# Four of sixteen scan inputs built by ScalarE and TensorE, more read-outs on GpSimd, and the z projection moved ahead of the gate

## The chip, the core and the metric

The kernel runs on one core of a Trainium2 chip. Five engines execute their own instruction streams and meet at semaphores: TensorE (PE in the profile, its weight loads PEld), VectorE (DVE), ScalarE (ACT), GpSimd (POOL) and SyncE (SP, which issues most DMAs). The metric is the device time of one execution in microseconds (us), lower is better. Before the change, three runs gave 1917.44, 1918.84 and 1922.55 us (median 1918.84).

## The reference, cut to what matters

Two layers, each a mixing block and a feed-forward block, work on x of shape (4, 256, 32, 32): 4 batches of 1024 tokens with 256 channels. The part that the change touches is the first mixing block. It cuts the 256 channels into 4 chunks of 64 and runs a state-space scan with 128 inner channels and 16 states over the 1024 tokens of each chunk of each batch:

```
xi, z = split(x @ in_proj.T);  xc = silu(causal_conv4(xi))
dbc = xc @ x_proj.T;  B, C = dbc[4:20], dbc[20:36]          # 16 numbers each per token
dt  = softplus(dbc[0:4] @ dt_proj.T + bias);  A = -exp(A_log)
h_t[d,s] = exp(dt_t[d] * A[d,s]) * h_(t-1)[d,s] + (dt_t[d] * xc_t[d]) * B_t[s]
y_t[d]   = sum_s h_t[d,s] * C_t[s];   out = ((y + xc * D) * silu(z)) @ out_proj.T
```

Behind it stand a projection, a quantized feed-forward layer, a group norm with channel attention, and at the end, over all 4096 tokens, a mixture of 8 experts with 2 chosen per token.

## The kernel before, in words

The program has three parts: four batches one after the other, then the routing, then the experts. A batch b has a stage of scans; the stage between two batches finishes batch b-1 (projection to gate) and begins batch b (convolution, dt, B and C, z). The first batch has a stage `start` in place of this.

**A scan.** Channels lie on the 128 partitions, the 1024 tokens along the free axis. One chunk has 16 states, a batch 64, numbered i = 0 to 63 (chunk i // 16, state s = i % 16). For each state four things are made, each of 128x1024 fp32: ScalarE writes the decay exp(dt * A) into PSUM (`decay`, L1002; two slots); GpSimd multiplies dt * xc with the row B[s], which SyncE has broadcast to all partitions by a DMA from the DRAM scratch `bc_rows` (`drive`, L1090; the product is called a drive here, three slots, the row buffers have four); VectorE runs the recurrence over both (`tensor_tensor_scan`, L1401; three state slots); then the state is multiplied with the row C[s] (the read-out, two slots `HC`) and TensorE adds the product into a PSUM bank by a matmul with the identity (`sum_states`).

**Read-outs** of states 2, 6, 10 and 14 are done by GpSimd with a C row broadcast by a DMA (L1098). The other twelve are done by VectorE (L1411) with a C row that TensorE spreads over the partitions into the one PSUM buffer `crep`: two bf16 matmuls (`c_row`) with a selector against `BCS`, which holds C as three bf16 parts that add up to the fp32 value. GpSimd makes these parts (`split_bc`), and SyncE copies them into place with 12 DMAs (`spread_bc`).

**Order.** Each engine runs its own list, written by loops over i. VectorE: scan i, at s = 1 and 2 of a later chunk the gating and the skip sum of the chunk before, read-out i-1. GpSimd: drive i, read-out i-2 where it is its own; beside that a few steps for dt of chunks 2 and 3 (`steps_of_dt`, after drives 2 and 8), a small norm step that waits for VectorE (`first_shift`, i = 35), and four bias sums (`residual`). TensorE: `c_row(i)`, `sum_states(i-1)`. ScalarE: decay i, then pieces of the norms of the last and the next batch. SyncE: row i of B, row i of C for GpSimd, and at i = 8 and 10 the store of the previous batch's tokens, a wait for it, and the load of the next batch.

**Between batches.** TensorE ends with `out_linear`, two transposes of the tokens (`tm_turn`), the gate's matmuls (`gate`) and only then the projection of z (`z_pair`, two halves). ScalarE runs the silu of z (`silu_z`, L829) inside the scans, after decay 1, which waits for the gate's logits (`gate_done`). VectorE computes `log1p` for chunks 0 to 3, the last one behind the logits (`route`). TensorE begins the scans when all of silu(z) is there.

Of the kernel before, what the change touches and what calls it, by code (L numbers as in the profile page):

```python
# [8 lines left out]
BF16 = mybir.dt.bfloat16  # L9
# [16 lines left out]
POOL_READS = (2, 6, 10, 14)  # L26
# [31 lines left out]
def on_pool(i):  # L58
    return i % NS in POOL_READS

# [27 lines left out]
def build_front(nc, t, out, xm_rows, bc_rows, logits, routing, experts):  # L88
    with ExitStack() as ctx:
# [76 lines left out]
        diag_d = shared(P)  # L166
        ffn_w = shared(CT, C)
# [16 lines left out]
        YF = shared(L)  # L184
        assert place[0] <= LAST_W2
# [36 lines left out]
        BC_REST = flat_rows(junk)  # L222
# [32 lines left out]
        dt_done = sem("dt_done"); dtx_done = sem("dtx_done"); bc_copy = sem("bc_copy"); bc_split = sem("bc_split"); bc_spread = sem("bc_spread")  # L255
        brow_ready = sem("brow_ready"); brow_stored = sem("brow_stored")
        b_loaded = [sem(f"b_loaded{k}") for k in range(B_SLOTS)]
        drive_ready = sem("drive_ready"); da_ready = sem("da_ready"); h_ready = sem("h_ready")
        crep_ready = sem("crep_ready"); c_loaded_rows = [sem(f"c_loaded_rows{k}") for k in range(2)]
# [5 lines left out]
        stats_there = sem("stats_there"); rest_there = sem("rest_there"); tokens_there = sem("tokens_there")  # L265
# [34 lines left out]
        def _(sp):  # L300
# [56 lines left out]
            for i in range(NI):  # L357
# [48 lines left out]
        def _(pe):  # L406
# [1617 lines left out]
```

## Time and profile before

| | |
|---|---|
| median of the runs shown | 1918.84 us |
| the profiled execution | 1918.7 us, its span 1916.9 us |
| scans of batches 0 to 3 | 83.9 to 296.1, 394.8 to 611.5, 712.9 to 929.0, 1030.3 to 1246.0 us |
| stages between | 98.7, 101.4, 101.3 us |
| after the last scan, to the first expert matmul | 1246.0 to 1396.8 us |
| experts | 1396.8 us to the end, PE busy 508.63 of 520.10 us |
| busy over the span | PE 79%, DVE 66%, POOL 60%, ACT 40% |

A scan stage is counted here from the start of the first scan to the end of the last read-out. In the second batch its chunks begin at about 394.8, 452.7, 504.9 and 558.7 us. In a row of windows the columns are start and end, length, then busy us of PE, PEld, DVE, ACT and POOL (in brackets the instructions), TensorE's granted clock as a share of its 2.4 GHz, the DMA engines' mean busy share and GB/s. In a timeline row the columns are start, duration, engine, line, operation, tiles, and in brackets the idle time ahead of it and what ended that. Many tiles share one SBUF buffer, which the trace calls `experts_sb`. A transpose on TensorE is a matmul of line 411; an fp32 matmul shows as two records.

### The profile page before, as it was taken

The page shows a single profiled execution, that of the slowest core. Times are in us where ns is not written, and L with a number is a line of the kernel's source. Part 1 is how long each engine was busy: PE and PEld are TensorE (multiplying, and loading weights), DVE is VectorE, ACT ScalarE, POOL GpSimd, SP SyncE. Part 2 cuts the span into 40 slices and gives each one's busy share as a digit, 9 for nine tenths or more (in the row PEclk, how much of TensorE's full clock was granted, in tenths as well). Part 3 has the DMA queues.
Part 4 walks back from the last instruction along what each step waited for, and adds up shares of the span by engine and source line. Part 5 has one row for each costly group of instructions (what it writes and reads, how often), then busy time and mean ns, then how long its engine had stood idle before and what let it go on. Part 6 is the DMA issues. An engine that isn't in the chain of part 4 may idle for free. (4 is left out here: it accounts for less than half of the span.)

```text
span 1916.9 us, 20726 instructions
## 1 busy us (share of the span) xinstructions
PE 1523.3 (79%) x5841; PEld 932.5 (49%) x5842; DVE 1258.3 (66%) x1415; ACT 772.8 (40%) x1218; POOL 1144.1 (60%) x602
## 2 busy tenths in 40 slices
PE   5567778957777877777896777767289999999997
PEld 2222225612223542222453222245178888888897
DVE  3589997589998678999848999963822222222222
ACT  7735435744443764543385344332022212222122
POOL 0799880479896068989217999800055455555543
PEclk9799999979999989999998999988589999999999
DMA  3365540146563036565004755481012222222222
GB/s 99 133 238 196 197 176 1 60 177 254 178 217 101 1 131 233 193 204 200 26 12 150 285 195 200 143 350 55 15 39 39 33 39 38 33 38 38 35 32 28
DMA packets 80689, 230.64 MB, mean 120 GB/s; under 512 B 12845, under 2 KB 31606, under 8 KB 77271
## 3 DMA queue, kind: packets, MB, share of 16 engines
q1 hardware_dynamic: 64694, 210.93, 31.1%
q0 software_dynamic: 15904, 18.66, 6.1%
q8 instruction: 38, 0.62, 0.1%
q14 instruction: 53, 0.43, 0.1%
HBM read 208.15 MB, written 19.82 MB: 119 GB/s over the span
## 5 line engine op out<-in xcount | busy, mean ns | idle before, releaser
L408 PE MATMUL psum<-HC_sb,ident_sb 128*128 128x512 f32 x1024 | 502.3, 616 | 98.7 <-DVE HC_sb L1411 50.2
L1002 ACT ACTIVATE psum<-experts_sb 128x1024 f32<-128x1024 f32 x256 | 285.2, 1117 | 492.4 <-DVE experts_sb L1401 363.5
L408 PE MATMUL psum<-experts_sb 64*128 64x512 f32 (+5 forms) x962 | 308.1, 551 | 180.1 <-DVE HC_sb L1411 100.2
L1401 DVE TENSOR_TENSOR_SCAN experts_sb<-psum,DBX_sb 128x1024 f32<-128x1024 f32 x172 | 389.8, 2278 | 36.9 <-POOL DBX_sb L1090 26.7
L408 PEld LDWEIGHTS psum<-HC_sb,ident_sb 128*128 128x128 f32 x1024 | 190.7, 194 | 323.6 <-issue 134.3
L408 PEld LDWEIGHTS psum<-experts_sb 64*128 64x128 f32 (+5 forms) x962 | 97.1, 153 | 418.6 <-DVE HC_sb L1411 191.3
L1817 ACT ACTIVATE hgt_sb<-psum_moe,b_sb 128x256 f32<-128x256 f32 (+1 forms) x312 | 116.2, 455 | 380.2 <-PE psum_moe L1724 380.2
L1969 DVE TENSOR_TENSOR YS_sb<-psum_moe,b_sb 128x256 f32<-128x256 f32 x71 | 30.2, 425 | 354.4 <-PE psum_moe L1724 354.4
L1724 PE MATMUL psum_moe<-XGT_sb,w1s_sb 128*128 128x256 f32 (+1 forms) x1248 | 254.7, 363 | 0.0
L1701 POOL DMA_INDIRECT out<-YS_sb,scat_sb x71 | 130.8, 1842 | 204.5 <-DVE YS_sb L1973 189.3
L1724 PE MATMUL psum_moe<-experts_sb,hgt_sb 128*128 x1136 | 251.7, 379 | 0.7 <-DVE YS_sb L1969 0.7
L1411 DVE TENSOR_TENSOR HC_sb<-psum,experts_sb 128x1024 f32<-128x1024 f32 x192 | 230.6, 1201 | 17.9 <-PE psum L408 17.7
L1724 PEld LDWEIGHTS psum_moe<-XGT_sb,w1s_sb 128*128 128x128 f32 x1248 | 219.4, 192 | 25.5
L1724 PEld LDWEIGHTS psum_moe<-experts_sb,hgt_sb 128*128 128x128 f32 x1136 | 215.2, 190 | 30.1 <-issue 1.1
L1090 POOL TENSOR_TENSOR DBX_sb<-DA_sb,experts_sb 128x1024 f32<-128x1024 f32 x88 | 209.7, 2385 | 7.0 <-DMA DA_sb<-bc_rows 7.0
L1401 DVE TENSOR_TENSOR_SCAN experts_sb<-psum,SQ_sb 128x1024 f32<-128x1024 f32 x84 | 191.1, 2275 | 2.9 <-POOL SQ_sb L1090 2.9
L1056 POOL TENSOR_TENSOR experts_sb<-experts_sb 128x1024 f32<-128x1024 f32 x16 | 38.6, 2412 | 243.3 <-DVE XSUM_sb L1292 181.3
L1689 POOL DMA_INDIRECT XG_sb<-xm_rows,tab_sb x71 | 70.6, 995 | 165.8 <-DMA gate_rows<-p21t_sb 144.4
L1098 POOL TENSOR_TENSOR HC_sb<-X_XT_sb,experts_sb 128x1024 f32<-128x1024 f32 x56 | 131.6, 2349 | 40.9 <-PE psum L408 40.6
L1090 POOL TENSOR_TENSOR DBX_sb<-SQ_sb,experts_sb 128x1024 f32<-128x1024 f32 x44 | 103.5, 2352 | 19.4 <-DMA SQ_sb<-bc_rows 19.3
L1090 POOL TENSOR_TENSOR DBX_sb<-experts_sb 128x1024 f32<-128x1024 f32 x40 | 94.2, 2355 | 0.0
L1090 POOL TENSOR_TENSOR SQ_sb<-DA_sb,experts_sb 128x1024 f32<-128x1024 f32 x40 | 94.2, 2354 | 0.0
(287 smaller groups left out, 1642.8 us busy)
## 6 DMA issues: line engine op xcount, KB each, us to landing
DA_sb<-bc_rows SPq DMA_DIRECT2D x128, 512.0 KB, 4.0
experts_sb<-bc_rows SPq DMA_DIRECT2D x64, 512.0 KB, 4.3
SQ_sb<-bc_rows SPq DMA_DIRECT2D x64, 512.0 KB, 5.1
X_XT_sb<-bc_rows SPq DMA_DIRECT2D x56, 512.0 KB, 5.5
experts_sb<-w1T SPq DMA_DIRECT2D x8, 1024.0 KB, 18.6
experts_sb<-w2T SPq DMA_DIRECT2D x8, 1024.0 KB, 20.6
X_sb<-x_tok SPq DMA_DIRECT2D x5, 1024.0 KB, 7.2
T_sb<-bc_rows SPq DMA_DIRECT2D x8, 512.0 KB, 6.3
```

The source lines that it names most:

```text
L408: return nc.tensor.matmul(o, lhsT, rhs, start=start, stop=stop, **k)
L1002: nc.scalar.activation(decays[i % 2], DT[:, c, :], ACT.Exp, scale=a_neg[:, s:s + 1]).then_inc(da_ready, 1)
L1056: nc.gpsimd.tensor_tensor(DT[:, c, :], DTX[:, c, :], log_tile(c), ALU.add).then_inc(dt_done, 1)
L1090: nc.gpsimd.tensor_tensor(DRIVE[i % STATE_SLOTS], B_REP[k], DTX[:, c, :], ALU.mult).then_inc(drive_ready, 1)
L1098: nc.gpsimd.tensor_tensor(HC[:, i % 2, :], c_rep(q), STATE[i % STATE_SLOTS], ALU.mult).then_inc(pool_read, 1)
L1401: v.tensor_tensor_scan(STATE[i % STATE_SLOTS], decays[i % 2], DRIVE[i % STATE_SLOTS], 0.0, ALU.mult, ALU.add).then_inc(h_ready, 1)
L1411: v.tensor_tensor(halves(HC[:, i % 2, :]), crep, halves(STATE[i % STATE_SLOTS]), ALU.mult).then_inc(dve_read, 1)
L1689: pool.indirect_dma_start(XG[:, k, :], None, xm_rows, bass.IndirectOffsetOnAxis(ap=TAB[:, tile:tile + 1], axis=0)).then_inc(xg_ready[k], 16)
L1701: pool.indirect_dma_start(out, bass.IndirectOffsetOnAxis(ap=SCAT[:, tile:tile + 1], axis=0), YS[:, tile % 4, :], None, compute_op=ALU.add) ...
L1724: return nc.tensor.matmul(o, lhsT, rhs, start=start, stop=stop, **k)
L1817: m = nc.scalar.activation(HGT[:, k, 4 * h + q, 0:w], psum[:, 2 * h + q // 2, (q % 2) * 2 * P:(q % 2) * 2 * P + w], ACT.Gelu, bias=b1[:, b ...
L1969: v.tensor_tensor(ys.unsqueeze(1), psum[:, 4 + j, 0:C].unsqueeze(1), b2[:, bass.ds(e, 1), :], ALU.add).then_inc(y_biased, 1)
```

## The change

1. **Turned drives.** For states 6, 9, 12 and 15 of each chunk (`TURNED_DRIVES`) the drive isn't made by GpSimd. Once per chunk TensorE transposes dt * xc into tokens-by-channels (`dtx_turn`, into the `crep` banks, at s = 2), and ScalarE copies it to SBUF (`dtx_tokens`). For each such state ScalarE scales the 8 blocks of 128x128 with the B value of each token (`scale_blocks`, spread behind the decays by the table `SCALED_AT`), and TensorE transposes them back into the PSUM slot of a decay (`turned_drive`, issued two states ahead). The decay of such a state goes to SBUF, so that the scan reads its decay from SBUF and its drive from PSUM. B is taken from a transpose of the B and C rows (`bc_turn`, `bc_tokens`). 16 B-row DMAs per batch go.
2. **Read-outs.** GpSimd takes 5, 6, 7 and 7 of the 16 read-outs of chunks 0 to 3 in place of 4 each (`POOL_READS`), 25 a batch in place of 16.
3. **B and C split in PSUM.** The three bf16 parts are ScalarE's copies of the PSUM banks, with TensorE subtracting each part there by a matmul with a negative identity (`bc_minus`). GpSimd's three `split_bc` instructions go.
4. **z** is projected before and after the two token transposes, ahead of the gate's matmuls, with its silu around the token copies, ahead of the scans.
5. **Smaller moves.** `log1p` of chunk 3 before the logits; GpSimd's steps of dt for chunk 2 wait until all four `log1p` are done, and those of chunk 3 come at i = 9; the load of B row 3 is issued ahead of SyncE's wait for the logits; `c_row(0)` ahead of the first matmuls of a batch; the residual load and sums some states later.

```diff
-POOL_READS = (2, 6, 10, 14)
+POOL_READS = ((2, 8, 10, 12, 14), (2, 6, 8, 10, 12, 14), (2, 4, 6, 8, 10, 12, 14), (2, 4, 6, 8, 10, 12, 14))
+TURNED_DRIVES = (6, 9, 12, 15)
+SCALED_AT = {6: ((4, 4), (5, 4)), 9: ((6, 2), (7, 3), (8, 3)), 12: ((9, 2), (10, 3), (11, 3)), 15: ((12, 2), (13, 3), (14, 3))}
...
+            def bc_minus(b, q):
+                pe.wait_ge(bc_part, b * 3 + q + 1)
...
+                    i = mm(psum[:, 6 + h, :], minus_b[:, :], BC_PARTS[q][:, h * HL:(h + 1) * HL], False, q == 1,
...
                 attend(p)
-                out_linear(p)
+                if go_on:
+                    bc_turn(b)
+                    bc_minus(b, 0)
+                out_linear(p, (0, 1, 2))
+                if go_on:
+                    bc_minus(b, 1)
+                out_linear(p, (3,))
+                if go_on:
+                    z_pair(b, 0)
                 tm_turn(p, 0)
                 tm_turn(p, 1)
+                if go_on:
+                    z_pair(b, 1)
                 gate(p)
-                if go_on:
-                    z_pair(b, 0)
-                    z_pair(b, 1)
-                pe.wait_ge(gate_done, p + 1)
...
+                def turned_drive(i):
+                    c, k = i // NS, i % 2
+                    pe.wait_ge(h_ready, b * NI + (i - 1))
+                    pe.wait_ge(scaled, b * turned_drives(NI) + turned_drives(i) + 1)
+                    for n in range(NB):
+                        m = turn(psum[:, 2 * k + n // 4, (n % 4) * P:(n % 4 + 1) * P], scaled_tile(c)[:, n, :])
...
+                    if i + 2 < NI and is_turned(i + 2):
+                        turned_drive(i + 2)
+                    if i % NS == TOK_AT:
+                        dtx_turn(c)
                     c_row(i)
...
-                    nc.scalar.activation(decays[i % 2], DT[:, c, :], ACT.Exp, scale=a_neg[:, s:s + 1]).then_inc(da_ready, 1)
+                    nc.scalar.activation(DECAY_SB if is_turned(i) else decays[i % 2], DT[:, c, :], ACT.Exp, scale=a_neg[:, s:s + 1]).then_inc(da_ready, 1)
...
+                                    m = nc.scalar.activation(scaled_tile(c)[:, n, :], DTX_TOK[:, n, :], ACT.Copy,
+                                                             scale=B_TOK[:, n, c, k:k + 1])
...
                 for i in range(NI):
                     decay(i)
-                    if i == 1 and after:
-                        silu_z(b, 0)
-                        silu_z(b, 1)
-                        nc.scalar.preload_act_table_set(EXP_LN)
+                    if i % NS == TOK_AT + 2:
+                        dtx_tokens(i // NS)
...
+                    scale_blocks(i)
...
                     if i == STATE_SLOTS - 1:
+                        pool.wait_ge(sp_step, (b + 1) * (NC * SP_STEPS))
                         steps_of_dt(b, 2)
-                    if i == 8:
+                    if i == TURNED_DRIVES[1]:
                         steps_of_dt(b, 3)
```

GpSimd in the third chunk of the first batch (from i = 35 on; line 1090 is a drive, line 1098 a read-out, line 1077 `first_shift`), before:

```order
L1077 TENSOR_TENSOR experts_sb<-experts_sb 128x8
L1090 TENSOR_TENSOR DBX_sb<-DA_sb,experts_sb 128x1024
L1098 TENSOR_TENSOR HC_sb<-X1_XT_sb,experts_sb 128x1024
L1090 TENSOR_TENSOR DBX_sb<-DA_sb,experts_sb 128x1024
L1090 TENSOR_TENSOR SQ_sb<-experts_sb 128x1024
L1090 TENSOR_TENSOR DBX_sb<-SQ_sb,experts_sb 128x1024
L1090 TENSOR_TENSOR DBX_sb<-DA_sb,experts_sb 128x1024
```

The same place now (line 1209 is a drive, line 1217 a read-out, line 1193 `first_shift`):

```order
L1193 TENSOR_TENSOR experts_sb<-experts_sb 128x8
L1209 TENSOR_TENSOR DBX_sb<-DA_sb,experts_sb 128x1024
L1217 TENSOR_TENSOR HC_sb<-X1_XT_sb,experts_sb 128x1024
L1209 TENSOR_TENSOR SQ_sb<-DA_sb,experts_sb 128x1024
L1217 TENSOR_TENSOR HC_sb<-X1_XT_sb,experts_sb 128x1024
L1209 TENSOR_TENSOR DBX_sb<-experts_sb 128x1024
L1209 TENSOR_TENSOR DBX_sb<-SQ_sb,experts_sb 128x1024
```

Where four drives stood between two read-outs, one or two stand now: a second read-out (state 36) follows the drive of state 37, and no drive is made for state 38.

TensorE in the first chunk of the first batch (line 408 a matmul: `psum<-experts_sb` of 512 columns is a C row, `psum<-HC_sb` a sum), from the sums of states 0 and 1 on, before:

```order
L408 MATMUL psum<-HC_sb,ident_sb 128x512 x4
L408 MATMUL psum<-experts_sb 128x512 x2
L408 MATMUL psum<-HC_sb,ident_sb 128x512 x2
L408 MATMUL psum<-experts_sb 128x512 x2
L408 MATMUL psum<-HC_sb,ident_sb 128x512 x2
```

The same place now (line 443 a matmul, line 446 a transpose):

```order
L443 MATMUL psum<-HC_sb,ident_sb 128x512 x2
L446 MATMUL psum<-ident_sb,experts_sb 128x128 x8
L443 MATMUL psum<-HC_sb,ident_sb 128x512 x2
L443 MATMUL psum<-experts_sb 128x512 x2
L443 MATMUL psum<-HC_sb,ident_sb 128x512 x2
L446 MATMUL psum<-ident_sb,experts_sb 128x128 x8
L443 MATMUL psum<-experts_sb 128x512 x2
L443 MATMUL psum<-HC_sb,ident_sb 128x512 x2
```

Eight transposes stand ahead of the sum of state 1 (`dtx_turn`) and eight ahead of the C row of state 4 (`turned_drive` for state 6): that row and the sums behind it now wait in TensorE's list for ScalarE's blocks.

ScalarE at the end of the stage between (line 844 and 846 the rsqrt of the token norm, 902 a token copy, 1002 a decay, 829 silu of z), before:

```order
L846 ACTIVATE token_rs_sb<-token_std_sb 128x4
L902 ACTIVATE T_sb<-psum 128x2x512
L1002 ACTIVATE psum<-experts_sb 128x1024 x2
L829 ACT_TABLE_LOAD
L829 ACTIVATE experts_sb<-psum 128x512 x4
L825 ISA
L829 ACTIVATE experts_sb<-psum 128x512 x4
L1009 ACT_TABLE_LOAD
```

Now (941 the rsqrt, 997 the token copies, 1108 a decay, 924 silu of z):

```order
L941 ACTIVATE token_rs_sb<-token_std_sb 128x4
L924 ACT_TABLE_LOAD
L924 ACTIVATE experts_sb<-psum 128x512 x4
L997 ACTIVATE T_sb<-psum 128x2x512 x2
L920 ISA
L924 ACTIVATE experts_sb<-psum 128x512 x4
L1091 ACT_TABLE_LOAD
L1108 ACTIVATE psum<-experts_sb 128x1024 x2
```

The silu of z and its two table loads stand ahead of the first decay now, not behind the second.

## Rows read from the trace of the kernel before

**Rows 1.** Windows: three scan stages, and the first two chunks of the second batch

```profile
83.90:296.10 212.20, 153.35 (x370) 58.16 (x370) 202.55 (x119) 84.75 (x107) 193.25 (x87) 0.97 0.54 193
394.80:611.50 216.70, 162.67 (x384) 60.59 (x384) 202.67 (x119) 93.20 (x123) 187.93 (x84) 0.95 0.57 200
712.90:929.00 216.10, 160.60 (x384) 59.99 (x384) 202.47 (x119) 93.20 (x123) 187.90 (x84) 0.96 0.57 200
394.80:452.70 57.90, 42.37 (x92) 15.58 (x92) 47.96 (x28) 27.35 (x39) 46.22 (x20) 0.86 0.67 252
452.70:504.90 52.20, 39.31 (x98) 14.43 (x96) 51.11 (x31) 27.17 (x46) 49.84 (x25) 1.00 0.57 194
```

**Rows 2.** Timeline of DVE inside a scan stage

```profile
287.80 1.20 DVE L1411 TENSOR_TENSOR HC_sb<-psum,experts_sb 128x1024 f32<-128x1024 f32 x1
288.91 2.28 DVE L1401 TENSOR_TENSOR_SCAN experts_sb<-psum,SQ_sb 128x1024 f32<-128x1024 f32 x1
```

**Rows 3.** Timeline of DVE at the start of the second batch's scans

```profile
394.81 4.47 DVE L1401 TENSOR_TENSOR_SCAN experts_sb<-psum,DBX_sb 128x1024 f32<-128x1024 f32 x2 [0.29 <-DVE experts_sb L1158]
404.97 1.22 DVE L1411 TENSOR_TENSOR HC_sb<-psum,experts_sb 128x1024 f32<-128x1024 f32 x1 [5.70 <-PE psum L408]
...
430.14 2.29 DVE L1401 TENSOR_TENSOR_SCAN experts_sb<-psum,DBX_sb 128x1024 f32<-128x1024 f32 x1 [3.02 <-POOL DBX_sb L1090]
...
443.74 2.29 DVE L1401 TENSOR_TENSOR_SCAN experts_sb<-psum,DBX_sb 128x1024 f32<-128x1024 f32 x1 [1.21 <-POOL DBX_sb L1090]
```

**Rows 4.** Timeline of DVE ahead of them: log1p of chunks 2 and 3

```profile
379.53 2.16 DVE L1155 SCALAR_TENSOR_TENSOR experts_sb<-experts_sb 128x1024 f32<-128x1024 f32 x1
381.73 3.26 DVE L1158 SCALAR_TENSOR_TENSOR experts_sb<-experts_sb 128x1024 f32<-128x1024 f32 x1
...
392.04 1.21 DVE L1155 SCALAR_TENSOR_TENSOR experts_sb<-experts_sb 128x1024 f32<-128x1024 f32 x1
```

**Rows 5.** Timeline of ACT in the stage between, to the first decays

```profile
366.31 1.02 ACT L801 ACTIVATE experts_sb<-psum 128x1024 f32<-128x1024 f32 x1
...
392.15 1.12 ACT L1002 ACTIVATE psum<-experts_sb 128x1024 f32<-128x1024 f32 x1 [9.91 <-DVE logits_sb L1362]
393.29 1.28 ACT L829 ACT_TABLE_LOAD   x1
394.58 2.06 ACT L829 ACTIVATE experts_sb<-psum 128x512 f32<-128x512 f32 x4
```

**Rows 6.** Timeline of PE: a transpose, a C row, sums at both clocks

```profile
347.18 1.04 PE L411 MATMUL psum<-ident_sb,X_XT_sb 128*128 128x128 f32 x8
...
415.06 0.60 PE L408 MATMUL psum<-experts_sb 128*128 128x512 bf16 x2 [1.36 <-DVE HC_sb L1411]
415.50 1.88 PE L408 MATMUL psum<-HC_sb,ident_sb 128*128 128x512 f32 x4
...
427.79 3.37 PE L408 MATMUL psum<-HC_sb,ident_sb 128*128 128x512 f32 x4 [3.69 <-POOL HC_sb L1098]
```

**Rows 7.** Timeline of ACT: the nearest to a 128x128 scaling

```profile
16.99 4.04 ACT L775 ACTIVATE X_sb<-X_sb,experts_sb 128x256 f32<-128x256 f32 x8 [0.62 <-POOL experts_sb L1077]
...
1861.25 1.14 ACT L1817 ACTIVATE hgt_sb<-psum_moe,b_sb 128x128 f32<-128x128 f32 x4 [7.83 <-PE psum_moe L1724]
```

**Rows 8.** Timeline of POOL: drives, a drive behind a late row, the norm step

```profile
202.73 0.20 POOL L1077 TENSOR_TENSOR experts_sb<-experts_sb 128x8 f32<-128x8 f32 x1 [5.38 <-DVE experts_sb L1149]
...
...
434.37 2.35 POOL L1090 TENSOR_TENSOR SQ_sb<-SQ_sb,experts_sb 128x1024 f32<-128x1024 f32 x1 [2.03 <-DMA SQ_sb<-bc_rows]
```

**Rows 9.** Timeline of SP: the token store and what follows it

```profile
419.39 0.41 SPq L313 DMA_DIRECT2D xm_rows<-X_XT_sb  x1
...
425.56 0.38 SPq L302 DMA_DIRECT2D X_sb<-x_tok  x1
426.21 0.33 SPq L336 DMA_DIRECT2D SQ_sb<-bc_rows  x1
```

**Rows 10.** Timeline of DVE: the first scan of the first batch

```profile
83.88 4.47 DVE L1401 TENSOR_TENSOR_SCAN experts_sb<-psum,DBX_sb 128x1024 f32<-128x1024 f32 x2 [8.34 <-ACT psum L1002]
```

More of the change, by code:

```diff
@@ L58, in on_pool, with is_turned, turned_drives, pool_drives @@
 def on_pool(i):
-    return i % NS in POOL_READS
+    return i % NS in POOL_READS[i // NS]
+def is_turned(i):
+    return i % NS in TURNED_DRIVES
+def turned_drives(i):
+    return sum(is_turned(j) for j in range(i))
+def pool_drives(i):
+    return i - turned_drives(i)
+def pool_driven(d):
+    return [j for j in range(NI) if not is_turned(j)][d]
+def rows_in_slot(k):
+    return sum(q % 2 == k for q in range(pool_reads(NI)))
 def pool_reads(i):
@@ L584, in attend, with out_linear @@
                 mm(psum[:, 0, 0:C], ones_row, bp_row, False, True).then_inc(fb_ready, 1)
-            def out_linear(p):
+            def out_linear(p, ks):
                 pe.wait_ge(f_done, p * 4 + 4)
-                for k, bank in enumerate(PO_BANKS):
+                for k in ks:
+                    bank = PO_BANKS[k]
                     if bank == 0:
@@ L689, in c_row, with dtx_turn @@
                     m.then_inc(crep_ready, 1)
+                def dtx_turn(c):
+                    i = c * NS + TOK_AT
+                    assert on_pool(i) and not on_pool(i + 1)
+                    pe.wait_ge(dtx_done, b * NC + c + 1)
+                    pe.wait_ge(dve_read, b * dve_reads(NI) + dve_reads(i))
+                    for n in range(NB):
+                        m = turn(psum[:, 4 + n // 4, (n % 4) * P:(n % 4 + 1) * P], DTX[:, c, n * P:(n + 1) * P])
+                    m.then_inc(tok_turned, 1)
+                def turned_drive(i):
+                    c, k = i // NS, i % 2
+                    pe.wait_ge(h_ready, b * NI + (i - 1))
+                    pe.wait_ge(scaled, b * turned_drives(NI) + turned_drives(i) + 1)
+                    for n in range(NB):
+                        m = turn(psum[:, 2 * k + n // 4, (n % 4) * P:(n % 4 + 1) * P], scaled_tile(c)[:, n, :])
+                    m.then_inc(turned_ready, 1)
                 def direct(c):
@@ L797, in read_dt, with bc_part_of @@
                 nc.scalar.activation(halves(DTX[:, c, :]), at, ACT.Relu, bias=dcols[:, 1:2]).then_inc(sp_relu, 1)
+            def bc_part_of(b, q):
+                if q:
+                    act.wait_ge(bc_rest, b * 2 + q)
+                nc.scalar.activation(halves(BC_PARTS[q]), psum[:, 6:8, :], ACT.Copy).then_inc(bc_part, 1)
             def read_bc(b):
@@ L801, in read_bc, with bc_tokens @@
                 nc.scalar.activation(halves(BCF), psum[:, 6:8, :], ACT.Copy).then_inc(brow_ready, 1)
-                nc.scalar.activation(halves(BC_PARTS[0]), psum[:, 6:8, :], ACT.Copy).then_inc(bc_copy, 1)
+                bc_part_of(b, 0)
+            def bc_tokens(b):
+                act.wait_ge(tok_turned, b * (NC + 1) + 1)
+                first, step = TURNED_DRIVES[0], TURNED_DRIVES[1] - TURNED_DRIVES[0]
+                at = psum[:, 4:6, :].rearrange("p g (n c k) -> p (g n) c k", n=4, c=NC)[:, :, :, first:NS:step]
+                nc.scalar.activation(B_TOK, at, ACT.Copy).then_inc(tok_copied, 1)
             def exp_of(b, c):
@@ L933, in start @@
                     logs_of(b, c)
+                    if c == 2:
+                        bc_tokens(b)
+                    bc_part_of(b, c - 1)
                 silu_z(b, 0)
@@ L981, in between @@
                         exp_of(b, c)
+                        if c == 2:
+                            bc_tokens(b)
+                        bc_part_of(b, c - 1)
                         logs_of(b, c)
+                token_rsqrt(p)
+                if go_on:
+                    silu_z(b, 0)
                 tm_copy(p, 0)
-                token_rsqrt(p)
                 tm_copy(p, 1)
-                if not go_on:
+                if go_on:
+                    silu_z(b, 1)
+                    nc.scalar.preload_act_table_set(EXP_LN)
+                else:
                     last_norm(p, range(NB))
```

124 lines of the change are left out of this document (82 added, 42 removed).

## The prediction

> **What bounds the kernel.** I read the table by engines first, then the windows over the scan stages. The last part, the experts, is TensorE's and the change leaves it alone, so what can move lies in the scan stages and the stages between. In a scan stage of a later batch VectorE is busy 202.7 of 216.7 us, GpSimd 187.9, TensorE 162.7, ScalarE 93.2 [rows 1]. VectorE is the bound, with GpSimd close behind: in the second chunk 51.11 and 49.84 of 52.20 us. The timeline of VectorE gives its prices: a scan follows the read-out before it after 1.11 us (287.80 to 288.91), though one takes 1.20 by itself, and a scan takes 2.28 [rows 2]. VectorE idles 216.7 - 202.67 = 14.0 us in that stage. Three waits make up 9.9 of it: 5.70 at the first read-out (TensorE starts only when all of silu(z) is there), 3.02 behind GpSimd's steps of dt for chunk 3, 1.21 for a late drive [rows 3]. The other 4.1 are small ones. In the first batch it idles 212.2 - 202.55 = 9.6 [rows 1].
>
> **What goes, per later batch.** GpSimd takes 25 read-outs in place of 16: 9 x 1.11 = 10.0 us off VectorE [rows 2]. The 5.70 wait goes nearly whole, since silu(z) is done ahead of the scans: 5.5. The 3.02 goes, since a steps pair now stands where GpSimd has fewer drives to make, and the 1.21, since the rows are fewer: 4.2. That wait had its origin on the queues: GpSimd waited 2.03 us for the row of a drive [rows 8], and this row was issued at 426.21 behind the token store at 419.39, the wait for it and the big load at 425.56 [rows 9]. Of the 4.1 of small waits I let 3.0 go, because a drive out of PSUM does not wait for GpSimd. Together 22.7.
>
> GpSimd's own list gets shorter too: 48 drives and 25 read-outs in place of 64 and 16, 7 x 2.35 = 16.5 us less [rows 8]. Its 187.9 becomes 171, and in the third and fourth chunk 19 operations x 2.35 = 45 us. It stays behind VectorE, whose second chunk goes from 51.11 to 51.11 - 2 x 1.11 = 48.9.
>
> **What comes: the turned drives.** Per chunk TensorE gets five groups of eight transposes at 1.04 = 5.2 us and loses two or three C rows at 0.45 to 0.60 [rows 6]: the second chunk's 39.31 becomes about 43.3. ScalarE gets 4 x 8 = 32 scalings of a 128x128 block by a per-partition value. The trace has no such instruction. From below, a gelu of 128x128 out of PSUM takes 1.14 / 4 = 0.29; from above, an activation of 128x256 takes 4.04 / 8 = 0.505 [rows 7]. The new form has the operand count of the second and the size of the first; I take the middle, 0.40, so 12.8 us a chunk, with 9.1 and 16.2 as ends. With one copy of the turned dt * xc (1.02, as the row at 366.31 [rows 5]) the second chunk's 27.17 [rows 1] becomes 41. At the upper end it is 44.4. All this lies beside VectorE's 49, but now four engines stand at 41 to 49 where one or two did, and they wait on each other in order: TensorE's transposes stand ahead of C rows and sums, wait for ScalarE's blocks and for the scan that frees the decay slot, and what is queued behind them are VectorE's C rows. There is one decay slot in SBUF and each turned drive holds one of two slots in PSUM, so ScalarE can run ahead less.
>
> No row shows these waits. From below they cost nothing, as when every part arrives two states early. From above they take back all that the read-outs and small waits give, that is a chunk stays as long as it was. I take a value nearer the lower end, by chunk: 4.5 us in the first (ScalarE comes late from the norm and has the dtx copy and four blocks to do before state 6: 1.0 + 4 x 0.40 = 2.6, less what is ahead; and the store, wait and load on SP still stand ahead of a row, 2.03 at 434.37 [rows 8], grown by GpSimd coming sooner), 2.0 in the second (ScalarE has the batch's sums beside the blocks), 3.0 in the third, 1.5 in the fourth. The 3.0 is for the small norm step on GpSimd: in the first batch it idled 5.38 us there for VectorE [rows 8], and where four drives followed it that fill the slots, a denser list with a read-out every second or third place follows now. Sum 11.0. So a later batch's scans change by -22.7 + 11.0 = -11.7.
>
> **The stage between.** The first scan starts at 394.81 [rows 3]. It waits for decay 0 (392.15, 1.12 long), which ScalarE ran after 9.91 us of idling for the logits, and VectorE's last log1p at 392.04 [rows 4, 5]. Now log1p of chunk 3 stands ahead of the logits, and ScalarE's idle time takes the silu of z and its two table loads (1.28 + 2.06 + 1.28 = 4.6 us). What holds the scan then is ScalarE's chain from 366.31 on, longer by the copies of the B and C parts (about 1.0 each by that row, between matmuls of TensorE), by the B tokens and by the silu. I put the first scan at 392.5, 2.3 earlier; the ends are 5.7 earlier (all of VectorE's logits and log1p work out of its way) and 2 later (every copy added). This is per later batch; the sum of a later batch is -14.0, of three -42.
>
> The order of log1p and drives is where a row bears on it: the log1p pair of chunk 2 took 2.16 + 3.26 us with drives 0 to 2 beside it on GpSimd, the one at 392.04 took 1.21 [rows 4]. If drives slow it again, the start is later by up to 5.42 - 2.42 = 3.0 us; this is inside the ends above.
>
> A scan of a turned state has its decay in SBUF and its drive in PSUM, which no row shows. The nearest rows have it the other way round and take 2.28 [rows 2]; the far end is the stretch of that log1p pair, 5.42 / 2.42 = 2.24, which would make it 5.1 and cost 2.8 x 16 = 45 us a batch. I take 2.28, for it still has one input in each memory as the scans with that time have, and give the far end no place in the range.
>
> The Trainium skill ("SBUF — State Buffer", "Who interferes with whom") says that a VectorE instruction with two SBUF inputs and a GpSimd instruction that reads SBUF shut one another out, and that one with a single SBUF input is not held up. By this rule a turned scan stays at 2.28 and the sum at -48; were the turned scans among those held up, it would be -48 + 4 x 45 = +132. The trace so far goes with the rule: log1p with two SBUF inputs was stretched, scans with one were not [rows 2, 4].
>
> **The first batch.** Read-outs give 10.0 as before; of its 9.6 us of idle I let 8.0 go. Against it: the scans begin after 8.34 us of waiting for ScalarE [rows 10], and that chain now holds the B tokens and two more copies of about 1.0, so 3.3 later; steps of dt for chunk 2 stand behind the log1p, 2.5; and 2.0, 3.0 and 1.5 as above. -18.0 + 12.3 = -6 (rounded).
>
> **Sum.** -42 - 6 = -48 against the profiled execution's 1918.7, which is within 0.2 us of the median 1918.84: 1918.7 - 48 = 1870.7, so 1870.
>
> **Rivals.** *VectorE alone sets the pace.* The new waits come to 1 us a chunk. Then a later batch gives 22.7 - 4 + 2.3 = 21.0, three 63; the first 18.0 - 4 - 3.3 - 2.5 = 8.2: 71 in all, 1848. For it speaks that GpSimd falls to 45 and TensorE stays at 43 of a 49 us chunk; against it that ScalarE's part may be near 44 and that TensorE's order ties the four together.
>
> *The chunks after the first keep their lengths.* What is taken off VectorE comes back as waits for TensorE's turned drives and GpSimd's read-outs; only the z wait, the start and 1 us go: 8.8 x 3 = 26, the first batch nothing, 1892. For it speaks that GpSimd was only 1.3 us behind VectorE in the second chunk [rows 1], and that each of 16 turned drives a batch is a new meeting of ScalarE, TensorE and VectorE; against it that they are issued two states, some 6 us, ahead.
>
> *TensorE becomes the bound, slower than before.* After a wait of 3.69 us a sum took 3.37 in place of 1.88 us [rows 6], 1.79 times as long: the granted clock fell to its lower level (1.2 GHz) there, and the first chunk's mean is 0.86 against 1.00 in the second [rows 1]. If transposes waiting for ScalarE make such gaps in every chunk and a share f of its work is done at the lower level, a chunk takes 43.3 x (1 + 0.79 f). It passes the old mean of 216.1 / 4 = 54.0 at f = 0.31; at 0.35 it is 55.3, +1.3 for twelve chunks and +2.2 for the first batch's four (53.05): +24, less 7 for the start and plus 3.3: about 1939. Against it: clock 1.00 in the second chunk though TensorE was idle a quarter of it. The Trainium skill ("TensorE: Matmul & The Clock Gate", "Part 4: PE-mode transpose") says that transposes don't bring up the full clock; here sums stand between them, 30 of 43 us, and no row shows the mixture.
>
> *It does not reach the end.* Gains and waits cancel: within 0.3% (5.8 us, about what a measurement of this kernel can tell from no change) of the old time.
>
> **How the numbers follow.** Forecast 0.44, VectorE alone 0.22, chunks keep their lengths 0.18, TensorE the bound 0.10, cancelled 0.06. Faster by over 0.3% is 0.44 + 0.22 + 0.18 = 0.84, within it 0.06, slower 0.10. The forecast's own range is 1858 to 1884: the block price's ends (3.4 to 3.7 us of ScalarE's time a chunk, of which a quarter shows: 0.9 x 16 = 14) and the start's. The range goes below 1848 by the start's lower end (3.4 x 3 = 10) and some of the waits, to 1832, and above 1892 by 10, to 1902; left out are the last two cases and the edges of the others.
>
> **What would show it.** VectorE's 5.70 us ahead of the first read-out is gone; a later scan stage is about 205 us long with VectorE busy 192.5 and GpSimd 171; scalings last 0.29 to 0.505; scans of turned states last 2.28; the second batch's first scan stands 2.3 us nearer to the end of the first batch's scans, the first batch's own at about 87; TensorE's granted clock stays at 0.95. I am wrong if VectorE shows waits for TensorE over 1 us in most chunks, if turned scans are stretched, if the clock of a later chunk falls under 0.9, or if ScalarE is busy over 45 us in a chunk.

## The result: 1 per cent faster, half of what was forecast

Six runs of the changed kernel took 1882.99 to 1908.48 us, median 1896.65; six of the kernel before, in the same two sets, 1917.44 to 1922.55, median 1919.58. The ratio is 0.9876, 95% interval 0.9845 to 0.9907. The forecast was 1870 in a range of 1832 to 1902: the sign is right and the time lies in the range, but the gain is 23 us where 48 were forecast.

The profiled execution took 1894.62 us (span 1892.8), 24.1 less than that of before. By stage, from the starts of the first and last scans in the trace, rounded to 0.1 us; a stage is taken to end 3.3 us, the pace of a state, behind the start of its last scan:

| | before | forecast | measured |
|---|---|---|---|
| first scan of the first batch | 83.9 | +3.3 | +1.9 |
| scan stage, first batch | 211.6 | -9.0 | -6.3 |
| scan stages, later batches | 216.2, 215.6, 215.2 | -11.7 each | -5.6, -6.9, -4.9 |
| stages between | 99.3, 101.9, 101.8 | -2.3 each | +1.3, -2.8, -3.2 |
| after the last scan | 671.4 | 0 | +2.4 |

So the scan stages gave 23.7 us where 44.1 were forecast. These 20.4 us are most of the 23.6 that are missing in all.

### The profile page after: what moved, and what is told of

The parts are those of the page before. It is cut to its first block and busy times, and to the rows that moved or that the text cites. A ratio compares the mean times of both kernels' runs of the same rounds, so it can differ in the third digit from the quotient of the medians.

```text
span 1892.8 us, 22487 instructions
## 1 busy us (share of the span) xinstructions
PE 1585.9 (84%) x6457; PEld 1005.2 (53%) x6458; DVE 1194.8 (63%) x1380; ACT 946.7 (50%) x1758; POOL 1047.3 (55%) x562
## 5 line engine op out<-in xcount | busy, mean ns | idle before, releaser
L443 PE MATMUL psum<-experts_sb 64*128 64x512 f32 (+5 forms) x906 | 285.4, 545 | 81.1 <-DVE experts_sb L1564 25.6
L1108 ACT ACTIVATE psum<-experts_sb 128x1024 f32<-128x1024 f32 x192 | 212.7, 1112 | 225.9 <-DVE experts_sb L1527 113.4
L1527 DVE TENSOR_TENSOR_SCAN experts_sb<-psum,DBX_sb 128x1024 f32<-128x1024 f32 x128 | 290.1, 2281 | 54.6 <-POOL DBX_sb L1209 40.8
L1217 POOL TENSOR_TENSOR HC_sb<-X_XT_sb,experts_sb 128x1024 f32<-128x1024 f32 x80 | 188.6, 2358 | 39.3 <-PE psum L443 38.9
L1536 DVE TENSOR_TENSOR HC_sb<-psum,experts_sb 128x1024 f32<-128x1024 f32 x156 | 187.8, 1204 | 6.1 <-PE psum L443 5.8
L1209 POOL TENSOR_TENSOR DBX_sb<-DA_sb,experts_sb 128x1024 f32<-128x1024 f32 x64 | 150.7, 2357 | 55.5 <-DMA DA_sb<-bc_rows 54.2
L1124 ACT ACTIVATE experts_sb<-experts_sb 128x128 f32<-128x128 f32 x512 | 166.9, 388 | 26.0 <-PE psum L446 23.0
L1527 DVE TENSOR_TENSOR_SCAN experts_sb<-psum,SQ_sb 128x1024 f32<-128x1024 f32 x64 | 145.8, 2278 | 16.2 <-POOL SQ_sb L1209 13.6
L1527 DVE TENSOR_TENSOR_SCAN experts_sb<-experts_sb,psum 128x1024 f32<-128x1024 f32 x64 | 145.4, 2271 | 0.0
L446 PEld LDWEIGHTS psum<-ident_sb,experts_sb 128*128 128x128 f32 x672 | 77.2, 145 | 87.0 <-issue 46.8
```

The source lines that it names most:

```text
L443: return nc.tensor.matmul(o, lhsT, rhs, start=start, stop=stop, **k)
L446: return nc.tensor.transpose(o, src, ident[:, :])
L1108: nc.scalar.activation(DECAY_SB if is_turned(i) else decays[i % 2], DT[:, c, :], ACT.Exp, scale=a_neg[:, s:s + 1]).then_inc(da_ready, 1)
L1124: m = nc.scalar.activation(scaled_tile(c)[:, n, :], DTX_TOK[:, n, :], ACT.Copy, scale=B_TOK[:, n, c, k:k + 1])
L1209: nc.gpsimd.tensor_tensor(DRIVE[d % len(DRIVE)], B_REP[k], DTX[:, c, :], ALU.mult).then_inc(drive_ready, 1)
L1217: nc.gpsimd.tensor_tensor(HC[:, i % 2, :], c_rep(q), STATE[i % STATE_SLOTS], ALU.mult).then_inc(pool_read, 1)
```

## The profile after

Windows over the four scan stages; the columns are those of [rows 1]:

```profile
85.80:291.10 205.30, 166.54 (x509) 73.08 (x510) 192.59 (x110) 126.83 (x239) 180.35 (x81) 0.98 0.54 186
391.70:602.30 210.60, 172.32 (x513) 76.53 (x512) 192.25 (x110) 130.32 (x247) 172.49 (x77) 0.95 0.55 187
701.40:910.10 208.70, 167.95 (x512) 73.84 (x511) 192.53 (x110) 130.09 (x247) 173.10 (x78) 0.98 0.55 189
1008.70:1219.00 210.30, 169.33 (x511) 73.67 (x510) 192.17 (x110) 131.49 (x248) 172.62 (x78) 0.97 0.56 188
```

The busy times came out as worked out: in a later batch VectorE 192.3 (forecast 192.5), GpSimd 172.5 (171), and TensorE's granted clock is 0.95 to 0.98 over a stage. But VectorE idles 210.60 - 192.25 = 18.4 us in the second batch's stage, where it idled 14.0 [rows 1]. The new idle time is not where I looked for it. The groups of lines, whose last part is the idle time before them and what ended it, show a scaling, a turned scan, and whom the other scans wait for:

```profile
L1124 ACT ACTIVATE experts_sb<-experts_sb 128x128 f32<-128x128 f32 x512 | 166.9, 388 | 26.0 <-PE psum L446 23.0
L1527 DVE TENSOR_TENSOR_SCAN experts_sb<-experts_sb,psum 128x1024 f32<-128x1024 f32 x64 | 145.4, 2271 | 0.0
L1527 DVE TENSOR_TENSOR_SCAN experts_sb<-psum,DBX_sb 128x1024 f32<-128x1024 f32 x128 | 290.1, 2281 | 54.6 <-POOL DBX_sb L1209 40.8
```

A scaling takes 0.388 us by itself (0.40 was taken; four in a row take 1.28). No turned scan waits for anything: 0.0. The scans of the other states wait for GpSimd's drives, 40.8 us in this row and 13.6 in the one with `SQ`, 54.4 in all where it was 29.6 before. And GpSimd, ahead of its drives, waits for the rows of B. The lines of the drive (L1090 in the kernel before, then L1209 in the changed one) by what ended their idle time, us and times:

```profile
  DMA SQ_sb<-bc_rows: 24.5, 6
  DMA DA_sb<-bc_rows: 7.0, 1
```

```profile
  DMA DA_sb<-bc_rows: 76.4, 24
  DMA experts_sb<-bc_rows: 12.3, 15
```

Seven waits of 31.5 us before, 39 of 88.7 now. Four of them in either kernel (26.4 and 28.1 us) stand ahead of a scan stage or at its start; inside the stages three waits of 5.2 us became 35 of 60.6. The transfers are not more but fewer (48 + 25 rows a batch in place of 64 + 16); they are issued late, in three places.

The first is the token store. SyncE's list, GpSimd's and VectorE's rows there (the second batch's first chunk), each from the timeline of the changed kernel; the place of [rows 8, 9]. L344 is the token store, L333 the 1 MB load of the next batch, L376 a row of C, L367 a row of B:

```profile
415.65 0.41 SPq L344 DMA_DIRECT2D xm_rows<-X_XT_sb  x1
416.26 0.43 SPq L376 DMA_DIRECT2D T_sb<-bc_rows  x1
416.96 0.96 SPq L367 DMA_DIRECT2D DA_sb<-bc_rows  x1
421.31 0.33 SPq L376 DMA_DIRECT2D T_sb<-bc_rows  x1
421.84 0.33 SPq L333 DMA_DIRECT2D X_sb<-x_tok  x1
422.81 0.33 SPq L367 DMA_DIRECT2D DA_sb<-bc_rows  x1
```

```profile
423.88 2.34 POOL L1209 TENSOR_TENSOR SQ_sb<-DA_sb,experts_sb 128x1024 f32<-128x1024 f32 x1 [7.84 <-DMA DA_sb<-bc_rows]
...
431.17 2.35 POOL L1209 TENSOR_TENSOR DBX_sb<-DA_sb,experts_sb 128x1024 f32<-128x1024 f32 x1 [2.64 <-DMA DA_sb<-bc_rows]
```

```profile
426.26 2.29 DVE L1527 TENSOR_TENSOR_SCAN experts_sb<-psum,SQ_sb 128x1024 f32<-128x1024 f32 x1 [1.63 <-POOL SQ_sb L1209]
...
433.54 2.29 DVE L1527 TENSOR_TENSOR_SCAN experts_sb<-psum,DBX_sb 128x1024 f32<-128x1024 f32 x1 [3.88 <-POOL DBX_sb L1209]
```

The store waits until 415.65 for ScalarE's last norm of the tokens. The row for the drive of state 10 stands behind it: issued at 416.96, there at 423.88. The next is issued at 422.81 behind the 1 MB load and takes 8.4 us. GpSimd, which no longer makes the drive of states 6 and 9, comes to state 10 earlier than the kernel before did (24 us behind the first scan, not 35), and waits 7.84 us there and 2.64 us for state 11; before, it waited 2.03 us, for state 11 alone.

The second place is in the denser read-outs of the later chunks. GpSimd and SyncE in the third chunk of the second batch (L1217 is a read-out):

```profile
517.45 2.38 POOL L1209 TENSOR_TENSOR SQ_sb<-DA_sb,experts_sb 128x1024 f32<-128x1024 f32 x1
...
527.72 2.35 POOL L1217 TENSOR_TENSOR HC_sb<-X_XT_sb,experts_sb 128x1024 f32<-128x1024 f32 x1
530.04 2.34 POOL L1209 TENSOR_TENSOR SQ_sb<-DA_sb,experts_sb 128x1024 f32<-128x1024 f32 x1
532.35 2.34 POOL L1217 TENSOR_TENSOR HC_sb<-X_XT_sb,experts_sb 128x1024 f32<-128x1024 f32 x1
535.76 2.36 POOL L1209 TENSOR_TENSOR DBX_sb<-DA_sb,experts_sb 128x1024 f32<-128x1024 f32 x1 [1.06 <-DMA DA_sb<-bc_rows]
```

```profile
530.24 0.33 SPq L376 DMA_DIRECT2D X_XT_sb<-bc_rows  x1
530.83 0.33 SPq L367 DMA_DIRECT2D DA_sb<-bc_rows  x1
534.87 0.33 SPq L376 DMA_DIRECT2D X_XT_sb<-bc_rows  x1
```

The drive at 535.76 uses the second half of `DA`, which came free at 517.45 + 2.38 = 519.8. Its row is issued 11 us later, at 530.83, because a C row stands ahead of it in SyncE's list, and the slot of that C row comes free only when the read-out at 527.72 is over (530.07). Then it takes 4.9 us to land. The drive, of state 43, is 1.06 late, and VectorE waits 1.47 us at 538.15 for it.

The third place is new with the change: ahead of the second 1 MB load (L336), at state 16, SyncE now also waits for the turned drive of state 15 (TensorE's transposes, L446), since the first chunk's scaled blocks lie in the buffer that the load fills.

```profile
441.45 1.09 PE L446 MATMUL psum<-ident_sb,experts_sb 128*128 128x128 f32 x8 [0.29 <-DVE experts_sb L1527]
```

```profile
436.58 0.33 SPq L367 DMA_DIRECT2D DA_sb<-bc_rows  x1
442.80 0.33 SPq L336 DMA_DIRECT2D experts_sb<-x_tok  x1
443.39 0.33 SPq L367 DMA_DIRECT2D DA_sb<-bc_rows  x1
```

```profile
449.76 2.35 POOL L1209 TENSOR_TENSOR DBX_sb<-DA_sb,experts_sb 128x1024 f32<-128x1024 f32 x1 [2.38 <-DMA DA_sb<-bc_rows]
```

```profile
452.15 2.29 DVE L1527 TENSOR_TENSOR_SCAN experts_sb<-psum,DBX_sb 128x1024 f32<-128x1024 f32 x1 [2.04 <-POOL DBX_sb L1209]
```

SyncE waits 5.4 us for those transposes. The row of state 17, whose buffer came free at 431.17 + 2.35 = 433.5, is issued behind the load, at 443.39. This is the wait of VectorE at state 17. No run moves this load alone.

## The experiments

Theory: with GpSimd's fewer drives and denser read-outs, SyncE's single list of transfers sets when rows of B arrive, and through them the pace. Rival: the turned drives tie TensorE, ScalarE and VectorE together (the mechanism that the prediction priced). Medians, with the ratio to the kernel before in the same set; chunk lengths of the second batch in the profiled execution (from first scan to first scan, of rounded starts; the fourth to 3.3 us behind its last scan's start):

| kernel | us | ratio, 95% | chunks 1 to 4 |
|---|---|---|---|
| before | 1919.58 | 1 | 57.8, 52.2, 53.8, 52.4 |
| changed | 1896.65 | 0.9876 (0.9845 to 0.9907) | 55.0, 51.6, 53.1, 50.9 |
| e1 token store later | 1877.29 | 0.9772 (0.9752 to 0.9792) | 48.1, 51.8, 53.0, 50.7 |
| e2 rows of B ahead | 1851.08 | 0.9637 (0.9620 to 0.9654) | 48.9, 49.8, 51.3, 49.1 |
| e3 both | 1848.77 | 0.9620 (0.9604 to 0.9636) | 48.2, 49.7, 51.3, 49.1 |
| e4 no turned drives, 4 reads | 1915.33 | 0.9969 (0.9956 to 0.9983) | 54.6, 53.5, 53.8, 52.4 |
| e5 turned, 4 reads | 1900.56 | 0.9911 (0.9882 to 0.9939) | 53.3, 52.4, 53.3, 52.5 |
| e6 before, rows of B ahead | 1914.94 | 0.9967 (0.9956 to 0.9978) | 56.6, 52.3, 53.8, 52.4 |
| e7 e5 with rows ahead | 1885.34 | 0.9817 (0.9795 to 0.9839) | 49.4, 51.7, 53.3, 52.5 |
| e8 e3, norm step later | 1839.02 | 0.9586 (0.9561 to 0.9611) | 47.8, 49.7, 49.2, 49.1 |
| e9 e4 with rows ahead | 1902.81 | 0.9908 (0.9886 to 0.9930) | 51.9, 53.5, 53.7, 52.4 |
| e10 e9 with 25 reads | 1958.94 | 1.0206 (1.0176 to 1.0236) | 50.5, 58.5, 58.3, 56.9 |

**e1, the token store later.**

```diff
-TOKENS_AT, NEXT_AT, X_AT, TOK_AT = 8, 10, 16, 2
+TOKENS_AT, NEXT_AT, X_AT, TOK_AT = 12, 14, 16, 2
```

> The changed kernel with one edit on SyncE's list: the store of the previous batch's tokens stands at state 12 in place of 8, the wait for it and the load of the next batch at 14 in place of 10. Theory (rows): in the first chunk of a later batch GpSimd waits 7.84 + 2.64 us for rows of B that stand in SyncE's list behind that store, and VectorE waits 1.63 + 3.88 us for these drives; the edit takes about 4 of the 5.5 us away in each of three batches, so about 12 us faster than the changed kernel, near 1884. Rival (coupling of TensorE and ScalarE by the turned drives): VectorE waits there for something else as soon as the rows are early, and the time stays within 4 us of 1896.

1877.29: 19 us less, for 12 expected. The first chunk of the second batch falls from 55.0 to 48.1 and the others stay; over the three later batches the first chunk falls by 6.0 us on average. The first place is shown, and what VectorE still waits for there is small: 0.72, 0.41 and 0.44 us for ScalarE and TensorE.

**e2, rows of B ahead of rows of C.**

```diff
+AHEAD = 2
...
+            for i in range(AHEAD):
+                load_b(0, i)
             for i in range(NI):
-                load_b(0, i)
+                if i + AHEAD < NI:
+                    load_b(0, i + AHEAD)
                 load_c(0, i)
...
-                    if i >= 4:
-                        load_b(b, i)
+                    if 4 <= i + AHEAD < NI:
+                        load_b(b, i + AHEAD)
```

> The changed kernel with one edit on SyncE's list: row i of C is issued behind row i+2 of B, not behind row i. Theory (rows): in the second to fourth chunks GpSimd waits some 1 us at a time for rows of B that stand behind a C row whose slot comes free only with GpSimd's own read-out two earlier, and VectorE waits 1.1 to 2.0 us at states 17, 43 and 59; 1 to 1.5 us a chunk go, about 12 us in all, near 1884. Rival (coupling): GpSimd has its rows but still runs into VectorE, the time stays within 4 us of 1896.

1851.08: 46 us less for the order of one engine's list alone. All four chunks fall, for the edit reaches all three places: the row of state 10 now also stands ahead of the token store, and that of state 17 ahead of the load. GpSimd's waits for rows of B fall to these, of which the four in the first line stand ahead of the scan stages:

```profile
  DMA DA_sb<-bc_rows: 28.2, 4
...
  DMA experts_sb<-bc_rows: 1.3, 2
```

and the second batch's stage reads

```profile
382.36:581.50 199.14, 164.56 (x504) 73.16 (x511) 192.15 (x110) 130.09 (x247) 173.03 (x78) 0.98 0.57 198
```

VectorE idles 7.0 us in place of 18.4, and every engine's work is the same. My size (12) was far too small: I had added up only the waits above 1 us of the three later chunks, and neither the token store nor the first batch, whose scan stage falls by 6.0. In the profiled executions some 40 of the 48 us between the two kernels are in the scan stages; of the rest, 3.1 are the stage between with the slower gate (below), and 3.4 behind the last scan stay unexplained.

**e3, both.**

> Both edits together. Theory (rows): the two gains add up, about 25 us faster than the changed kernel, near 1872, the time that the prediction gave. Rival (coupling): within 6 us of 1896.

1848.77. The gains don't add up, since e2 had the row of state 10 ahead of the store already. The whole gain on the change, 48 us, is nearly twice the 25 expected.

**e4, no turned drives.** `is_turned` returns False; the transposes, the copy of dt * xc and the scalings go (the turn of the B and C rows and its copy stay), and

```diff
-POOL_READS = ((2, 8, 10, 12, 14), ...)
+POOL_READS = ((2, 6, 10, 14),) * 4
```

> The changed kernel without turned drives (all 64 drives of a batch on GpSimd again, with the transposes, the copies and the scalings left out) and with 4 read-outs a chunk on GpSimd as before; z ahead of the gate, B and C split in PSUM and the smaller moves stay. Theory (rows): what stays is the z wait (5.5 a later batch) and the earlier start (2.5), 8 x 3 = 24 us, less the later start of the first batch and the longer tail, 4 to 5: near 1899, so the turned drives with the extra read-outs have given next to nothing by themselves. Rival (coupling): the turned drives hold the chunks up by themselves and this kernel is clearly faster than the changed one, near 1886.

1915.33, a miss for both. The turned drives and the read-outs together are worth 1915.33 - 1896.65 = 19 us, not next to nothing. The z wait of 5.70 us [rows 3] is gone, but the first chunk is 3.2 us shorter, not 5.5, the second is 1.2 longer and the first batch's stage 2.8 longer. VectorE's timeline in the first chunk shows what is late next:

```profile
427.80 2.29 DVE L1514 TENSOR_TENSOR_SCAN experts_sb<-psum,DBX_sb 128x1024 f32<-128x1024 f32 x1 [2.02 <-POOL DBX_sb L1196]
430.00 1.20 DVE L1523 TENSOR_TENSOR HC_sb<-psum,experts_sb 128x1024 f32<-128x1024 f32 x1
435.16 2.29 DVE L1514 TENSOR_TENSOR_SCAN experts_sb<-psum,DBX_sb 128x1024 f32<-128x1024 f32 x1 [3.96 <-POOL DBX_sb L1196]
```

At state 9 it waits 2.02 behind a row that stands behind the token store, at state 10 3.96 behind GpSimd's steps of dt for chunk 3. The z wait had been cover for GpSimd.

**e5, turned drives with 4 read-outs; e7, the same with rows ahead.** The edits are those of `POOL_READS` in e4, and for e7 that of e2 too.

> The changed kernel with GpSimd's read-outs put back to 4 a chunk (states 2, 6, 10, 14); turned drives and SyncE's list as in the change. Theory (rows): it is the denser read-outs that block SyncE's list, because the slot of a C row comes free two read-outs earlier, four states back in place of eight; so GpSimd's waits for rows go in the second to fourth chunks, but VectorE gets 9 read-outs x 1.11 = 10.0 us a batch back: 1897 - 33 (the row waits there) + 40 = about 1900, with the waits of the first chunk behind the token store still there. Rival (turned drives alone make GpSimd outrun its rows): the row waits stay in all chunks and the time is 1930 or more.

> The changed kernel with row i of C behind row i+2 of B, and 4 read-outs a chunk on GpSimd as before. Theory (with the rows in time VectorE sets the pace): each of the 9 x 4 read-outs given back costs VectorE 1.11 us, so 1851 + 40 = about 1891. Rival (GpSimd or TensorE sets the pace then): GpSimd has 9 x 2.35 us a batch less to do, and the time changes by less than 15 us from 1851.

1900.56 and 1885.34, close to the theory (1900 and 1891). With the change's order of rows the extra read-outs are worth 1900.56 - 1896.65 = 4 us, which is within the spread of these runs; with rows in time 1885.34 - 1851.08 = 34 us, of the 40 that VectorE is relieved of. In e5 the waits of VectorE at states 43 and 59 are gone; those at 10 and 11 (0.47 and 3.96), behind the store, and at 17 (0.92), behind the load, stay. So the denser read-outs make the C rows block the list.

**e6, the kernel before with rows ahead.** The edit of e2.

> The kernel before with the same edit on SyncE's list (row i of C behind row i+2 of B). Theory (the change made the row order a bound; before, GpSimd waited for a row only once a later batch, 2.03 us, and VectorE 1.21 us behind it): at most 3 x 1.2 = 4 us, between 1916 and 1921. Rival (the order was a bound all along and its mending has nothing to do with the change): 20 us or more faster than before.

1914.94, by the ratio 4 to 8 us faster than before: a little more than the theory's bound, and far from the rival. The same edit is worth 5 us ahead of the change and 46 behind it.

**e8, the norm step later.** On top of e3:

```diff
-                    if i == FIRST_AT + 2 * NB + NB // 2 + 1:
+                    if i == FIRST_AT + 2 * NB + NB // 2 + 3:
                         first_shift(b + 1)
```

> The kernel with both edits on SyncE's list, and GpSimd's small norm step (first_shift) two states later, after the drive of state 37 in place of 35. Theory: of VectorE's waits of 1.2 + 0.5 + 1.2 us at states 33, 36 and 37, the last two stand behind GpSimd's 4.9 us of waiting for that step, about 1.5 us a batch go, near 1843. Rival: drive slots hold GpSimd back there anyway, or ScalarE's norm is late next: 1847 to 1850.

1839.02, the fastest of all, 81 us under before. The third chunk goes from 51.3 to 49.2; the waits at states 36 and 37 are gone, that at 33 (1.2) stays.

```profile
379.90:575.70 195.80, 165.66 (x505) 73.26 (x512) 191.60 (x110) 129.77 (x247) 172.64 (x78) 0.98 0.60 202
```

VectorE idles 4.2 of 195.8 us in this stage.

**e9, e4 with rows ahead; e10, that with 25 read-outs.** The edit of e2 on e4; for e10 the change's `POOL_READS` as well.

> The kernel without turned drives and with 4 read-outs a chunk on GpSimd (z ahead of the gate, the split in PSUM and the smaller moves stay; the transposes, copies and scalings of the turned drives are left out), now with row i of C behind row i+2 of B. Theory (in that kernel the z wait turned into waits for GpSimd, which has no slack there: rows behind the token store, and 4.8 us for dt of chunk 3): the row part goes, 2 us a later batch, the dt part of 4.0 stays, so 1915 - 7 = about 1908, and a turned drive is then worth (1908 - 1885) / 64. Rival (the whole of the first chunk's wait stands behind the rows): 5 to 6 us a later batch, near 1897.

> The same kernel without turned drives and with row i of C behind row i+2 of B, but with the change's 25 read-outs a batch on GpSimd. Theory (the turned drives are what makes room for the read-outs): GpSimd has 64 drives and 25 read-outs, 89 x 2.33 = 207 us, and some 12 us of smaller steps in a scan stage: it sets the pace at about 220 us a stage, near 1930. Rival (read-outs help by themselves once the rows are in time): below 1900.

e9: 1902.81, between the two; the first chunk gains 2.7 us and a wait of 3.4 us at state 10, for dt, stays. With rows in time the turned drives alone are worth 1902.81 - 1885.34 = 17 us. e10: 1958.94, slower than before, as the theory had it though by more than its 1930. VectorE's work in the second batch's stage falls to 195.0, nearly as in the change, but GpSimd is busy 209 of 224 us:

```profile
415.50:639.70 224.20, 154.43 (x356) 58.95 (x356) 194.95 (x110) 89.07 (x115) 209.33 (x94) 0.96 0.63 213
```

Read-outs on GpSimd pay only when it is rid of drives. Together, with rows in time: 1903, with turned drives 1885, with read-outs too 1851; with read-outs alone 1959.

## Why the prediction was half right

- **What goes: right for VectorE's own work, wrong for the rows.** 9 read-outs of 1.11 us came off VectorE (busy 202.7 to 192.3), and the 5.70 us wait for z went. But the sentence "and the 1.21, since the rows are fewer" is the step that failed. I counted rows and not when they are issued. The 1.21 behind a late row became 1.63 + 3.88 in the first chunk, and 2.04, 1.47 and 1.54 us at states 17, 43 and 59.
- **The small waits.** I let 3.0 of their 4.1 us go, but 2.3 of them were at states 33, 36 and 37 (0.56, 0.53 and 1.21), which wait for drives that GpSimd still makes. They are 3.1 now.
- **What comes: wrong in its causes.** The 11.0 us a later batch were priced as 4.5 + 2.0 + 3.0 + 1.5, mostly for ScalarE's blocks, the norm step and TensorE's order. Measured: 22.7 - 5.8 (the mean gain of the three later stages) = 16.9. In e3, where the rows are in time, a later stage is 198.0 us, so that 22.7 - (215.7 - 198.0) = 5.0 came. The part of rows is thus 11.9 a later batch. Only the first chunk's term named SyncE's list; of its 4.5 ScalarE's blocks were at most 2.6, so it left some 2 us or more for the list, and e1 gives 6.0. The terms of the other chunks put late rows at nothing: the prediction did not ask what a C row waits for, nor the load at state 16. By VectorE's waits in e3 the other 5.0 are the small waits that stayed, 3.1, and some 2 us of waits for ScalarE and TensorE, 1.20 and 0.41 of them about state 5.
- **The first batch:** its stage gave 6.3 for 9.0. In e2 it gives 12.4, so late rows took 6 us here too.
- **The norm step: not a new cost.** Its 3.0 was for a wait that the change would lengthen. VectorE's waits at states 36 and 37, before and in the changed kernel, with GpSimd's at that step:

```profile
518.27 0.20 POOL L1077 TENSOR_TENSOR experts_sb<-experts_sb 128x8 f32<-128x8 f32 x1 [4.98 <-DVE experts_sb L1149]
```

```profile
520.88 2.29 DVE L1401 TENSOR_TENSOR_SCAN experts_sb<-psum,DBX_sb 128x1024 f32<-128x1024 f32 x1 [0.53 <-POOL DBX_sb L1090]
...
525.50 2.29 DVE L1401 TENSOR_TENSOR_SCAN experts_sb<-psum,DBX_sb 128x1024 f32<-128x1024 f32 x1 [1.21 <-POOL DBX_sb L1090]
```

```profile
512.38 0.20 POOL L1193 TENSOR_TENSOR experts_sb<-experts_sb 128x8 f32<-128x8 f32 x1 [4.91 <-DVE experts_sb L1270]
```

```profile
515.23 2.29 DVE L1527 TENSOR_TENSOR_SCAN experts_sb<-psum,DBX_sb 128x1024 f32<-128x1024 f32 x1 [0.66 <-POOL DBX_sb L1209]
...
519.86 2.29 DVE L1527 TENSOR_TENSOR_SCAN experts_sb<-psum,SQ_sb 128x1024 f32<-128x1024 f32 x1 [1.23 <-POOL SQ_sb L1209]
```

They are 1.74 and 1.89 us in sum. What e8 takes off, 2.1 us a batch, had been there before the change; the kernel before was not run with that edit.

- **The turned drives: right.** 0.388 us a block, the scan at 2.271, no turned scan late. TensorE as the bound, the rival with 0.10, didn't appear: TensorE was busy 42 of 51.6 us in the second chunk at a clock of 1.00. The rule of the Trainium skill ("SBUF — State Buffer", "Who interferes with whom"), that GpSimd does not hold up a VectorE instruction with at most one SBUF input (outside its 2-port modes), held for the turned scans: 2.271 us beside GpSimd's drives.
- **The start:** 85.8 for the forecast 87, and later stages between shorter by 2.8 and 3.2 for 2.3. The one ahead of the second batch grew by 1.3, since VectorE waited 7.36 us there for the gate's logits; in e2 that wait was 3.06. The gate's matmuls show why, in the second and the third batch of the changed kernel and in the second of e2:

```profile
384.15 6.99 PE L443 MATMUL psum<-gate_w_sb,T_sb 128*128 128x8 f32 x32
```

```profile
696.11 3.74 PE L443 MATMUL psum<-gate_w_sb,T_sb 128*128 128x8 f32 x32
```

```profile
377.12 3.74 PE L447 MATMUL psum<-gate_w_sb,T_sb 128*128 128x8 f32 x32
```

From 385 to 400 us the granted clock in the second batch of the changed kernel was 0.50, the lower of the two levels (1.2 GHz), and in e2 it was 1.00 over its gate. TensorE had idled 1.77 us ahead of the second half of z, as it did in the other two places, and why the clock fell in this one is open. It was 0.80 over the first chunk that followed, the one sign of being wrong that showed, but the kernel before had 0.86 there [rows 1]. Open, too, are the 2.4 us after the last scan, which e1 to e3 don't show.

- **The rivals:** "the chunks after the first keep their lengths" gave 1892 and was nearest, and in the second batch these chunks did shorten by only 0.6 to 1.5 us; but the mechanism was another than the one it named. "VectorE alone sets the pace" gave 1848: that is e3, the change without its row order.
- **The range** held the time by luck. It had been stretched to 1902 for that first rival; the forecast's own, 1858 to 1884, misses 1896.65.

## What to carry to other kernels

When an engine is relieved, follow every list that feeds it. SyncE's list had a critical order of its own here: a transfer whose buffer came free late held up all behind it. For each transfer ahead of a critical one, ask what its buffer or data waits for, and issue the critical one as soon as its own buffer is free. A part of a change that measures as worth nothing (here the read-outs, 4 us) can be worth 34 once the wait that it has run into is gone, so parts are best judged together with the lists that feed them.

## What the runs showed of the hardware

A row broadcast of 512 KB took 4.9 us from issue to the drive that uses it in the third chunk, 6.9 next to the token store and 8.4 behind a 1 MB load. A ScalarE scaling of a 128x128 fp32 block by a per-partition value took 0.388 us. The gate's matmuls (32 records) took 3.74 us at a granted clock of 1.00 and 6.99 at 0.50. The changed kernel's runs spread over 25 us (1882.99 to 1908.48), e3's over 3 (1846.82 to 1849.70): with the rows late, the spread of the times was almost nine times as wide. That the transfers' own spread is the cause was not tried.
